# Stage order and buffer depth in the edge score stage of a graph network kernel

## Chip, cores and metric

One core of one Trainium2 chip runs the whole kernel. The metric is device time in microseconds (us) of one execution; the number compared is the median of repeated runs.

## What is computed

The reference takes 50,000 nodes of 128 features and 25,000 edges through four graph layers. The part that matters here is the start of the third layer, an edge attention:

```python
x_norm = _layernorm(x, g1, be1)
q = (x_norm @ Wq + bq).reshape(num_nodes, NH, HD)
k = (x_norm @ Wk + bk).reshape(num_nodes, NH, HD)
v = (x_norm @ Wv + bv).reshape(num_nodes, NH, HD)
scores = jnp.einsum('ehd,ehd->eh', q[src], k[tgt]) / np.sqrt(HD).astype(np.float32)
scores = scores + (curv @ Wc + bc)
```

There are 8 heads of 16 features. `curv` is the edge attribute table, 25,000 rows of 128. The kernel fetches both end rows of each edge and does norm and projections per edge; nothing is computed per node and looked up later.

## The kernel before

The stage is `scores_phase` (L2301 to L2477). The edges are padded to 200 tiles of 128 and taken in 50 groups of four tiles (`GT = 4`, `EG = 50`). Each group goes through these steps:

- **Gather** (L2378, POOL): eight indirect DMAs fetch the source and the target rows of four tiles, each row in two halves of 128 features, into one of four slots (`SC = 4`) of `sc_rows`. Gather g waits until group g-4 has been added.
- **Add** (L2393, DVE): the halves are added into `sc_xin`, and `norm.statistics` (L1150 to L1163) makes mean and variance.
- **Root** (L1171, ACT), then **normalise** (L1176, L1183, DVE): reciprocal and eight tensor_scalar into `sc_xn`.
- **Turn** (L2448, L2450, PE): eight 128x128 transposes of `sc_xn` and four of the attribute rows, into three PSUM tiles `sc_t`. Then PE waits for its own transposes (L2452) and gives the attribute slot free (L2453).
- **Copy** (L2423, L2424, ACT): the three PSUM tiles go to SBUF.
- **Project** (L2473, L2463, L2467, PE): three biases and twelve 128x128 matmuls into query, key and value PSUM tiles `sc_o`, and the small attribute product. There is one set of these tiles, so project g+1 waits until group g is scored and its value is copied.
- **Values** (L2429, L2431, ACT): copy of query and of value.
- **Score** (L2403, L2406, L2409, DVE): query times key, sum by head, plus the attribute part.
- **Load and put** (L2343, L2359, SP): 256 KB of attribute rows in, 256 KB of values out. The attribute rows have two slots.

What sets the order is written out by hand. `pipeline` (L1883) runs ticks m = 0, 1, 2, and so on; in tick m each engine's program does its steps in the listed order, step s for group m minus the lag of s. Each engine then runs its list strictly in order, and semaphores join the engines. In the kernel before the lists are:

- DVE: normalise (lag 1), score (3), add (0)
- ACT: values (3), copy (1), root (0)
- PE: turn (1), project (2)
- SP: load (0), put (4)

After its own steps each engine also does a piece of `EdgeEnds` (L2480 to L2580) in its tick: small loads of ids and bias rows on SP in ticks 0 to 9, the filling of a table with bias rows from tick 12 on (two 512 KB DMAs per tick), and some masks on DVE, ACT and PE. The change leaves these as they are.

Of the kernel before, what the change touches and what calls it, by code (L numbers as in the profile page):

```python
# [20 lines left out]
P = 128  # L21
D = 128
# [2277 lines left out]

def scores_phase(k, o, ends):  # L2301
# [4 lines left out]
    with ExitStack() as st:  # L2306
        rows = k.sb(st, "sc_rows", [P, SC, C, 2 * D])
        attr = k.sb(st, "sc_attr", [P, 2, GT, D])
# [12 lines left out]
        names = ["attr0", "attr1", "attr_tail", "attr_free", "added", "normed", "turned", "copied",  # L2321
# [9 lines left out]
        def run(*stages):  # L2331
            pipeline(EG, *((lambda g, f=f: f(g, g // 2, g % 2, P), lag) for f, lag in stages))

        with nc.Block() as block:
            @block.sync
            def _(sp):
                edge_attr = k.a["edge_attr_128"]

                def load(g, i, u, p):
                    sp.wait_ge(s["attr_free"], g + 1)  # L2340
                    if not isinstance(g, int) or g < full:
                        at = slice(g * (GT * P), (g + 1) * (GT * P)) if isinstance(g, int) else bass.ds(g * (GT * P), GT * P)
                        sp.dma_start(attr[:, u, :, :], edge_attr[at, :].rearrange("(t p) d -> p t d", p=P))\  # L2343
                          .then_inc(s[f"attr{u}"], 16)
                    elif g == full:
# [6 lines left out]
                                     .rearrange("(t p) d -> p t d", p=P)).then_inc(s[f"attr{u}"], 16)  # L2352
                    else:
                        sp.sem_inc(s[f"attr{u}"], 16)

                def put(g, i, u, p):
                    sp.wait_ge(s["value"], g + 2)
                    at = slice(g * (GT * P), (g + 1) * (GT * P)) if isinstance(g, int) else bass.ds(g * (GT * P), GT * P)
                    sp.dma_start(k.values[at, 0:D].rearrange("(t p) d -> p t d", p=P), value[:, u, :, :])\  # L2359
                      .then_inc(s[f"value_put{u}"], 16)  # L2360

                sp.wait_ge(s["cleared"], 1)
                for u in range(2):
                    sp.sem_inc(s[f"value_put{u}"], 16)
                run((load, 0), (put, 4), (lambda g, i, u, p: ends.sync(g), 0))
                ends.close_sync()
                for u in range(2):
                    sp.wait_ge(s[f"value_put{u}"], 16 * (EG // 2) + 16)
# [15 lines left out]
            def _(dve):  # L2384
# [3 lines left out]
                dve.sem_inc(s["scored"], 1)  # L2388

                def add(g, i, u, p):  # L2390
# [7 lines left out]
                def normalise(g, i, u, p):  # L2398
                    norm.normalise(dve, g, u, P, xn[:, u, :, :], xin[:, u, :, :]).then_inc(s["normed"], 1)
# [1007 lines left out]
```

## Time and profile before

| what | value |
|---|---|
| median of 3 runs | 5611.9 us |
| lowest and highest | 5609.29 and 5619.23 us |
| span of the profiled execution | 5967.4 us |
| PE busy, share of the span | 3527.0 us, 59% |
| DVE busy, share | 3844.7 us, 64% |
| ACT busy, share | 2300.9 us, 39% |
| POOL busy, share | 3031.0 us, 51% |
| mean granted TensorE clock | 0.792 |

The span goes from the first to the last instruction. For the profiled execution no other time than its span is recorded; it is 355.5 us, or 6.3%, above the median of the runs without a profile. The busy shares are means over stages that differ, so they don't tell what bounds any one stage. The score stage takes from 2828.7 us to about 3526 us of the span, 12% of it.

### The profile page before, as it was taken

The numbers are of one execution on the slowest core, as the hardware profiler recorded it, in microseconds if no ns is written. First come the engines' busy times: TensorE is split into PE (matmuls) and PEld (weight loads), VectorE is DVE, ScalarE is ACT, GpSimd is POOL, SyncE is SP. The second block draws the span as 40 slices with busy tenths as digits, with TensorE's granted clock in tenths as the row PEclk, the third lists the DMA queues.
The fourth block names the chain that finished last, engine by engine and source line by source line (L and its number), as shares of the span: only waits on it lengthen the run. The fifth ranks groups of instructions, "written<-read, shape, count | busy, mean of one in ns | idle before, by whom it ended". The sixth has DMA issues, their size and how long they took to land. (4 is left out here: it accounts for less than half of the span.)

```text
span 5967.4 us, 70027 instructions
## 1 busy us (share of the span) xinstructions
PE 3527.0 (59%) x19808; PEld 2717.4 (46%) x19808; DVE 3844.7 (64%) x11203; ACT 2300.9 (39%) x5320; POOL 3031.0 (51%) x2733
## 2 busy tenths in 40 slices
PE   5677766267712466631455644444799993775443
PEld 1344445267611255531355542333577772664443
DVE  9666568379835466621465566666678882666998
ACT  0233330068810255521122222333466662334776
POOL 8666557625567422376655516776155555552000
PEclk9898887689955688965677776766899996997666
DMA  4455559479857777621455427777356653775554
GB/s 181 125 150 153 151 146 331 143 227 310 273 163 265 254 244 248 229 84 55 122 188 194 149 52 212 241 245 226 143 204 212 211 209 99 235 244 196 208 209 160
DMA packets 698336, 1147.11 MB, mean 192 GB/s; under 512 B 110368, under 2 KB 453459, under 8 KB 691702
## 3 DMA queue, kind: packets, MB, share of 16 engines
q1 hardware_dynamic: 594752, 959.48, 48.6%
q0 software_dynamic: 103200, 183.16, 10.5%
q8 instruction: 162, 2.65, 0.2%
q14 instruction: 222, 1.82, 0.1%
HBM read 689.93 MB, written 464.79 MB: 194 GB/s over the span
## 5 line engine op out<-in xcount | busy, mean ns | idle before, releaser
L2378 POOL DMA_INDIRECT sc_rows<-layer,node_idx x400 | 385.1, 963 | 264.3 <-DVE sc_xin L2393 135.6
L2252 PE MATMUL ro_end<-vals,end_mask 128*2 128x128 f32 x1600 | 243.0, 317 | 388.4 <-DVE vals L2116 243.2
L778 PE MATMUL msg_acc<-msg_pair,msg_vals 128*128 128x512 f32 (+3 forms) x400 | 210.2, 699 | 310.8 <-issue 147.5
L2903 POOL DMA_INDIRECT tf_edge_x<-y,tf_src_idx x200 | 198.0, 990 | 382.9 <-SPq L2879 334.2
L208 POOL DMA_INDIRECT x_src<-in_x_dram,node_idx x200 | 329.7, 1649 | 81.6 <-issue 60.7
L3049 PE MATMUL tf_o_ps<-pre_w,tf_hidden 128*128 128x128 f32 (+1 forms) x3136 | 362.2, 276 | 5.8 <-issue 5.2
L2252 PEld LDWEIGHTS ro_end<-vals,end_mask 128*2 128x2 f32 x1600 | 148.3, 96 | 474.0 <-DVE vals L2116 252.0
L3037 PE MATMUL tf_h_ps<-tf_x_t,pre_w 128*128 128x512 f32 x784 | 350.2, 600 | 19.1 <-ACT tf_hidden L2997 18.0
L3049 PEld LDWEIGHTS tf_o_ps<-pre_w,tf_hidden 128*128 128x128 f32 (+1 forms) x3136 | 356.6, 192 | 7.7 <-issue 7.6
L2278 PE MATMUL ro_acc<-vals,ro_mask 128*126 128x128 f32 x1600 | 240.4, 314 | 201.6 <-ACT ro_square L2210 87.0
L1611 POOL DMA_INDIRECT cap_own<-layer,w_own x200 | 204.5, 1022 | 292.2 <-SPq L1591 242.1
L2997 ACT ACTIVATE tf_hidden<-tf_h_ps,pre_b 128x512 f32<-128x512 f32 x392 | 269.1, 687 | 159.5 <-PE tf_h_ps L3037 119.3
L401 POOL DMA_INDIRECT agg<-rank_sums,d_last x200 | 211.5, 1058 | 227.0 <-ACT rank_sums L494 173.5
L2278 PEld LDWEIGHTS ro_acc<-vals,ro_mask 128*126 128x126 f32 x1600 | 222.3, 223 | 223.4 <-issue 188.3
L2066 POOL TENSOR_TENSOR vals<-ro_both,ro_weight 126x1024 f32<-126x1024 f32 x75 | 145.0, 1933 | 344.1 <-ACT ro_weight L2234 258.7
L1114 PE MATMUL ml_conv_out<-pre_mean_wt,ml_conv_tsb 128*128 128x128 f32 (+1 forms) x784 | 176.6, 417 | 231.4 <-DVEq L3221 226.8
L698 POOL DMA_INDIRECT msg_rows<-values,s_eid x200 | 217.9, 1090 | 186.9 <-POOLq L70 126.2
L778 PEld LDWEIGHTS msg_acc<-msg_pair,msg_vals 128*128 128x128 f32 x400 | 115.7, 304 | 402.8 <-issue 247.2
L893 POOL DMA_INDIRECT agg<-mean_sums,d_last x200 | 208.7, 1043 | 177.4 <-ACT mean_sums L938 128.3
L1114 PEld LDWEIGHTS ml_conv_out<-pre_mean_wt,ml_conv_tsb 128*128 128x128 f32 (+1 forms) x784 | 164.8, 319 | 244.5 <-issue 238.7
L1521 POOL DMA_INDIRECT sorted<-payload,rank x200 | 233.0, 1165 | 77.5 <-issue 64.2
L2079 POOL DMA_INDIRECT layer<-ro_far,w_last x200 | 215.8, 1079 | 105.0 <-issue 60.0
(487 smaller groups left out, 11220.1 us busy)
## 6 DMA issues: line engine op xcount, KB each, us to landing
ro_mask<-masks SPq DMA_DIRECT2D x100, 504.0 KB
layer<-zeros SPq DMA_DIRECT2D x96, 512.0 KB
si_both<-layer SPq DMA_DIRECT2D x48, 1024.0 KB
ro_far<-far SPq DMA_DIRECT2D x75, 512.0 KB
ro_both<-both SPq DMA_DIRECT2D x75, 512.0 KB
agg<-zeros SPq DMA_DIRECT2D x48, 512.0 KB
mom_x<-in_x_dram SPq DMA_DIRECT2D x48, 512.0 KB
mom_agg<-agg SPq DMA_DIRECT2D x48, 512.0 KB
```

The lines of the kernel that those rows point to most:

```text
L208: k.nc.gpsimd.indirect_dma_start(out=rows[:, t, :], out_offset=None, in_=k.x, in_offset=bass.IndirectOffsetOnAxis(ap=k.node_idx[:, 0, t:t ...
L698: nc.gpsimd.indirect_dma_start(out=rows[:, g % SS, j, :], out_offset=None, in_=table, in_offset=bass.IndirectOffsetOnAxis(ap=order.eid[:, ...
L778: mm = nc.tensor.matmul(acc[g % 3][:, i:GT, :].rearrange("p t e -> p (t e)"), vals[:, u, i, :], pair[:, u, FIRST[i]:FIRST[i] + GT - i, :]. ...
L1114: mm = self.k.nc.tensor.matmul(self.out[b][0:p, j, :], self.turned_sb[:, 4 * b + j, 0:p], self.weight, start=plain, stop=plain or j == 3, ...
L1521: k.nc.gpsimd.indirect_dma_start(out=k.sorted4[:, :], out_offset=bass.IndirectOffsetOnAxis(ap=k.rank[:, t:t + 1], axis=0), in_=k.payload[: ...
L2079: nc.gpsimd.indirect_dma_start(out=k.layer1_halves, out_offset=bass.IndirectOffsetOnAxis(ap=wide.last[real, t:t + 1], axis=0), in_=sent[re ...
L2252: mm = nc.tensor.matmul(end_ps[0:2, j, :], k.end_mask[:, t, :], k.vals[:, t, :], start=True, stop=True, skip_group_check=True)
L2278: mm = nc.tensor.matmul(acc[w][real, j, :], mask[:, u, j, :], k.vals[:, tile(n, j), :], start=True, stop=True, skip_group_check=True)
L2378: nc.gpsimd.indirect_dma_start(out=rows[:, g % SC, c * GT + j, :], out_offset=None, in_=k.layer1, in_offset=bass.IndirectOffsetOnAxis(ap=k ...
L2997: nc.scalar.activation(hidden[:, h, b, :], h_ps[b][:, :], ACT.Relu, bias=b1[:, b:b + 1]).then_inc(s["bent"], 1)
L3037: nc.tensor.matmul(h_ps[b][:, :], w1[:, b * P:(b + 1) * P], x_t[:, u, 4 * h:4 * h + 4, :].rearrange("p j e -> p (j e)"), start=True, stop= ...
L3049: mm = nc.tensor.matmul(o_ps[h][0:p, j, :], hidden[:, h, b, j * P:j * P + p], w2[:, b, :], start=b == 0, stop=b == NB - 1)
```

## The change

It touches only `scores_phase`. The lags become: DVE normalise 1, score 4, add 0; ACT values 4, copy 2, root 0; PE turn 2, project 3; SP load 0, put 5. So a group is turned in the tick after that in which it was normalised, and projected in the one after that. The attribute rows get four slots (`AS = 4`) with a semaphore each. A load now waits on `turned` directly, so PE's wait for its own transposes and the semaphore `attr_free` go. Normalise g gets a wait for turn g-2, which the old order implied; score also waits for `made`. Counts that were preset at the start (`value`, `copied`, `made`, `scored`, `value_put`) now start at zero.

```diff
--- before.py
+++ after.py
@@ -2298,6 +2298,9 @@
 Q = NH * CH
 
 
+AS = 4
+
+
 def scores_phase(k, o, ends):
 
 
@@ -2305,7 +2308,7 @@
     C = 2 * GT
     with ExitStack() as st:
         rows = k.sb(st, "sc_rows", [P, SC, C, 2 * D])
-        attr = k.sb(st, "sc_attr", [P, 2, GT, D])
+        attr = k.sb(st, "sc_attr", [P, AS, GT, D])
         xin = k.sb(st, "sc_xin", [P, 2, C, D])
         xn = k.sb(st, "sc_xn", [P, 2, C, D])
         x_t = k.sb(st, "sc_x_t", [P, 2, C, P])
@@ -2318,7 +2321,7 @@
         t_ps = [k.ps(st, f"sc_t{b}", [P, GT, P]) for b in range(3)]
         out_ps = [k.ps(st, f"sc_o{b}", [P, GT, D]) for b in range(3)]
         attr_ps = k.ps(st, "sc_attr_ps", [P, 512])
-        names = ["attr0", "attr1", "attr_tail", "attr_free", "added", "normed", "turned", "copied",
+        names = ["attr_in0", "attr_in1", "attr_in2", "attr_in3", "attr_tail", "added", "normed", "turned", "copied",
                  "made", "query", "value", "value_put0", "value_put1", "product", "dots", "scored", "cleared"]
         s = {x: k.sem(st, "sc_" + x) for x in names}
         ends.begin(st)
@@ -2328,20 +2331,18 @@
         full = E // (GT * P)
         assert full % 2 == 0 and full + 2 == EG
 
-        def run(*stages):
-            pipeline(EG, *((lambda g, f=f: f(g, g // 2, g % 2, P), lag) for f, lag in stages))
-
         with nc.Block() as block:
             @block.sync
             def _(sp):
                 edge_attr = k.a["edge_attr_128"]
 
-                def load(g, i, u, p):
-                    sp.wait_ge(s["attr_free"], g + 1)
-                    if not isinstance(g, int) or g < full:
-                        at = slice(g * (GT * P), (g + 1) * (GT * P)) if isinstance(g, int) else bass.ds(g * (GT * P), GT * P)
-                        sp.dma_start(attr[:, u, :, :], edge_attr[at, :].rearrange("(t p) d -> p t d", p=P))\
-                          .then_inc(s[f"attr{u}"], 16)
+                def load(g):
+                    u = g % AS
+                    if g >= AS:
+                        sp.wait_ge(s["turned"], g - AS + 1)
+                    if g < full:
+                        sp.dma_start(attr[:, u, :, :], edge_attr[g * (GT * P):(g + 1) * (GT * P), :]
+                                     .rearrange("(t p) d -> p t d", p=P)).then_inc(s[f"attr_in{u}"], 16)
                     elif g == full:
 
                         at, left = full * GT * P, E - full * GT * P
@@ -2349,23 +2350,20 @@
                           .then_inc(s["attr_tail"], 16)
                         sp.wait_ge(s["attr_tail"], 16)
                         sp.dma_start(attr[:, u, 0:left // P, :], edge_attr[at:at + left // P * P, :]
-                                     .rearrange("(t p) d -> p t d", p=P)).then_inc(s[f"attr{u}"], 16)
+                                     .rearrange("(t p) d -> p t d", p=P)).then_inc(s[f"attr_in{u}"], 16)
                     else:
-                        sp.sem_inc(s[f"attr{u}"], 16)
-
-                def put(g, i, u, p):
-                    sp.wait_ge(s["value"], g + 2)
-                    at = slice(g * (GT * P), (g + 1) * (GT * P)) if isinstance(g, int) else bass.ds(g * (GT * P), GT * P)
-                    sp.dma_start(k.values[at, 0:D].rearrange("(t p) d -> p t d", p=P), value[:, u, :, :])\
-                      .then_inc(s[f"value_put{u}"], 16)
+                        sp.sem_inc(s[f"attr_in{u}"], 16)
+
+                def put(g):
+                    sp.wait_ge(s["value"], g + 1)
+                    sp.dma_start(k.values[g * (GT * P):(g + 1) * (GT * P), 0:D].rearrange("(t p) d -> p t d", p=P),
+                                 value[:, g % 2, :, :]).then_inc(s[f"value_put{g % 2}"], 16)
 
                 sp.wait_ge(s["cleared"], 1)
-                for u in range(2):
-                    sp.sem_inc(s[f"value_put{u}"], 16)
-                run((load, 0), (put, 4), (lambda g, i, u, p: ends.sync(g), 0))
+                pipeline(EG, (load, 0), (put, 5), (ends.sync, 0))
                 ends.close_sync()
                 for u in range(2):
-                    sp.wait_ge(s[f"value_put{u}"], 16 * (EG // 2) + 16)
+                    sp.wait_ge(s[f"value_put{u}"], 16 * (EG // 2))
 
             @block.gpsimd
             def _(pool):
@@ -2385,78 +2383,78 @@
                 norm.prepare(dve)
                 nc.vector.memset(attr[:, :, :, :], 0.0).then_inc(s["cleared"], 1)
                 dve.wait_ge(s["cleared"], 1)
-                dve.sem_inc(s["scored"], 1)
-
-                def add(g, i, u, p):
-                    q = g % SC
+
+                def add(g):
+                    q, u = g % SC, g % 2
                     dve.wait_ge(k.gathered[q], in0[q] + (g // SC + 1) * 32 * GT)
                     nc.vector.tensor_tensor(xin[:, u, :, :], rows[:, q, :, 0:D], rows[:, q, :, D:2 * D],
                                             ALU.add).then_inc(s["added"], 1)
                     dve.wait_ge(s["added"], g + 1)
                     norm.statistics(dve, g, u, P, xin[:, u, :, :])
 
-                def normalise(g, i, u, p):
-                    norm.normalise(dve, g, u, P, xn[:, u, :, :], xin[:, u, :, :]).then_inc(s["normed"], 1)
-
-                def score(g, i, u, p):
+                def normalise(g):
+                    if g >= 2:
+                        dve.wait_ge(s["turned"], g - 1)
+                    norm.normalise(dve, g, g % 2, P, xn[:, g % 2, :, :], xin[:, g % 2, :, :]).then_inc(s["normed"], 1)
+
+                def score(g):
                     dve.wait_ge(s["query"], g + 1)
+                    dve.wait_ge(s["made"], g + 1)
                     nc.vector.tensor_tensor(terms[:, :, :], query[:, :, :], out_ps[1][:, :, :],
                                             ALU.mult).then_inc(s["product"], 1)
                     dve.wait_ge(s["product"], g + 1)
                     nc.vector.tensor_reduce(dots[:, :, :], terms[:, :, :].rearrange("p t (h d) -> p t h d", h=NH),
                                             AX.X, ALU.add).then_inc(s["dots"], 1)
                     dve.wait_ge(s["dots"], g + 1)
-                    nc.vector.tensor_tensor(k.scores[:, slice(g * GT, g * GT + GT) if isinstance(g, int) else bass.ds(g * GT, GT), :],
-                                            dots[:, :, :],
+                    nc.vector.tensor_tensor(k.scores[:, g * GT:(g + 1) * GT, :], dots[:, :, :],
                                             attr_ps[:, 0:GT * NH].rearrange("p (t h) -> p t h", h=NH),
                                             ALU.add).then_inc(s["scored"], 1)
 
-                run((normalise, 1), (score, 3), (add, 0), (lambda g, i, u, p: ends.vector(g), 0))
+                pipeline(EG, (normalise, 1), (score, 4), (add, 0), (ends.vector, 0))
 
             @block.scalar
             def _(act):
-                def copy(g, i, u, p):
+                def copy(g):
+                    u = g % 2
                     act.wait_ge(s["turned"], g + 1)
-                    if g:
-                        act.wait_ge(s["made"], g)
+                    if g >= 2:
+                        act.wait_ge(s["made"], g - 1)
                     for b in range(2):
                         nc.scalar.activation(x_t[:, u, b * GT:(b + 1) * GT, :], t_ps[b][:, :, :], ACT.Copy)
                     nc.scalar.activation(attr_t[:, u, :, :], t_ps[2][:, :, :], ACT.Copy).then_inc(s["copied"], 1)
 
-                def values(g, i, u, p):
-                    act.wait_ge(s["made"], g + 2)
-                    act.wait_ge(s["scored"], g + 1)
+                def values(g):
+                    u = g % 2
+                    act.wait_ge(s["made"], g + 1)
+                    if g:
+                        act.wait_ge(s["scored"], g)
                     nc.scalar.activation(query[:, :, :], out_ps[0][:, :, :], ACT.Copy).then_inc(s["query"], 1)
-                    act.wait_ge(s[f"value_put{u}"], i * 16 + 16)
+                    if g >= 2:
+                        act.wait_ge(s[f"value_put{u}"], g // 2 * 16)
                     nc.scalar.activation(value[:, u, :, :], out_ps[2][:, :, :], ACT.Copy).then_inc(s["value"], 1)
 
-                act.sem_inc(s["copied"], 1)
-                act.sem_inc(s["value"], 1)
-                run((values, 3), (copy, 1), (lambda g, i, u, p: norm.square_root(act, g, u, p), 0),
-                    (lambda g, i, u, p: ends.scalar(g), 0))
+                pipeline(EG, (values, 4), (copy, 2), (lambda g: norm.square_root(act, g, g % 2, P), 0), (ends.scalar, 0))
 
             @block.tensor
             def _(pe):
-                pe.sem_inc(s["made"], 1)
-                pe.sem_inc(s["attr_free"], 2)
-
-                def turn(g, i, u, p):
+                def turn(g):
+                    u, q = g % 2, g % AS
                     pe.wait_ge(s["normed"], g + 1)
-                    pe.wait_ge(s["copied"], g + 1)
-                    pe.wait_ge(s[f"attr{u}"], i * 16 + 16)
+                    if g:
+                        pe.wait_ge(s["copied"], g)
+                    pe.wait_ge(s[f"attr_in{q}"], g // AS * 16 + 16)
                     for j in range(C):
                         nc.tensor.transpose(t_ps[j // GT][:, j % GT, :], xn[:, u, j, :], k.ident[:, :])
                     for j in range(GT):
-                        mm = nc.tensor.transpose(t_ps[2][:, j, :], attr[:, u, j, :], k.ident[:, :])
+                        mm = nc.tensor.transpose(t_ps[2][:, j, :], attr[:, q, j, :], k.ident[:, :])
                     mm.then_inc(s["turned"], 1)
-                    pe.wait_ge(s["turned"], g + 1)
-                    pe.sem_inc(s["attr_free"], 1)
-
-                def project(g, i, u, p):
-                    pe.wait_ge(s["copied"], g + 2)
-
-                    pe.wait_ge(s["value"], g + 1)
-                    pe.wait_ge(s["scored"], g + 1)
+
+                def project(g):
+                    u = g % 2
+                    pe.wait_ge(s["copied"], g + 1)
+                    if g:
+                        pe.wait_ge(s["value"], g)
+                        pe.wait_ge(s["scored"], g)
                     for c in range(3):
                         add_bias(out_ps[c][:, :, :].rearrange("p t d -> p (t d)"), k.qkv_parts[c])
                         for j in range(GT):
@@ -2473,7 +2471,7 @@
                     nc.tensor.matmul(out, k.ones_bias[:, :], parts[:, :, :].rearrange("r t d -> r (t d)"), start=True,
                                      stop=False, skip_group_check=True)
 
-                run((turn, 1), (project, 2), (lambda g, i, u, p: ends.tensor(g), 0))
+                pipeline(EG, (turn, 2), (project, 3), (ends.tensor, 0))
         clear_semaphores(nc, norm.sems + list(s.values()) + ends.sems)
```

## Rows read from the trace of the kernel before

**Rows 1.** Busy time by engine (microseconds, instructions), granted clock, DMA share, score stage.

```profile
core 0: us, PE busy (x) PEld busy (x) DVE busy (x) ACT busy (x) POOL busy (x), PEclk, DMA share, GB/s
2835.00:3520.00 685.00, 390.28 (x2384) 354.34 (x2385) 379.64 (x1366) 150.77 (x302) 380.70 (x396) 0.74 0.49 153
```

**Rows 2.** The add of the two row halves: duration in ns, first and last start.

```profile
L2393 DVE TENSOR_TENSOR sc_xin<-sc_rows x50: 1216/1217/1226, 2840.9 to 3500.5; 128x1024 f32<-128x1024 f32 x50
```

**Rows 3.** Table of waits in the stage: total microseconds, times, longest.

```profile
ACT sc_query L2429 <- remote: 250.7, 34, 17.4
...
POOL sc_rows L2378 <- DVE sc_xin L2393: 135.6, 26, 11.8
...
PE sc_o L2473 <- remote: 117.3, 21, 9.1
```

**Rows 4.** Timeline: two gathers on POOL, eight apart (start, duration).

```profile
2833.21 0.95 POOL L2378 DMA_INDIRECT sc_rows<-layer,node_idx  x1 [0.30 <-issue]
...
2843.23 0.95 POOL L2378 DMA_INDIRECT sc_rows<-layer,node_idx  x1 [0.30 <-issue]
```

**Rows 5.** Timeline, middle of the stage: three groups on PE, ACT and DVE.

```profile
3278.40 1.08 ACT L2423 ACTIVATE sc_x_t<-sc_t 128x512 f32<-128x512 f32 x2 [5.32 <-remote]
...
3278.67 0.59 PE L2473 MATMUL sc_o<-pre_query_parts,ones_bias 128*128 128x512 bf16 x1 [6.73 <-remote]
...
3280.43 2.14 DVE L1183 TENSOR_SCALAR sc_xn<-sc_xin,sc_norm_mean,sc_norm_scale 128x128 f32<-128x128 f32 x8
...
3287.82 0.60 ACT L2429 ACTIVATE sc_query<-sc_o 128x512 f32<-128x512 f32 x1 [7.66 <-remote]
...
3288.94 1.08 ACT L2423 ACTIVATE sc_x_t<-sc_t 128x512 f32<-128x512 f32 x2
...
3290.00 1.22 DVE L2393 TENSOR_TENSOR sc_xin<-sc_rows 128x1024 f32<-128x1024 f32 x1
...
3290.23 0.59 PE L2473 MATMUL sc_o<-pre_query_parts,ones_bias 128*128 128x512 bf16 x1 [1.32 <-DVE scores L2409]
...
3297.57 0.60 PE L2450 MATMUL sc_t<-ident,sc_attr 128*128 128x128 f32 x4
...
3298.59 0.60 ACT L2429 ACTIVATE sc_query<-sc_o 128x512 f32<-128x512 f32 x1 [4.45 <-remote]
...
3304.29 1.08 ACT L2423 ACTIVATE sc_x_t<-sc_t 128x512 f32<-128x512 f32 x2 [4.61 <-remote]
...
3304.56 0.58 PE L2473 MATMUL sc_o<-pre_query_parts,ones_bias 128*128 128x512 bf16 x1 [6.39 <-remote]
...
3314.41 0.60 ACT L2429 ACTIVATE sc_query<-sc_o 128x512 f32<-128x512 f32 x1 [8.37 <-remote]
```

**Rows 6.** Timeline, end of the stage, after the last gather.

```profile
3492.53 1.22 DVE L2393 TENSOR_TENSOR sc_xin<-sc_rows 128x1024 f32<-128x1024 f32 x1
...
3492.76 0.38 PE L2473 MATMUL sc_o<-pre_query_parts,ones_bias 128*128 128x512 bf16 x1 [0.54 <-DVE scores L2409]
...
3497.18 0.60 ACT L2429 ACTIVATE sc_query<-sc_o 128x512 f32<-128x512 f32 x1 [0.51 <-PE sc_attr_ps L2467]
...
3500.06 0.60 PE L2450 MATMUL sc_t<-ident,sc_attr 128*128 128x128 f32 x4
...
3500.53 1.22 DVE L2393 TENSOR_TENSOR sc_xin<-sc_rows 128x1024 f32<-128x1024 f32 x1
3500.70 1.09 ACT L2423 ACTIVATE sc_x_t<-sc_t 128x512 f32<-128x512 f32 x2 [2.43 <-PE sc_t L2450]
```

**Rows 7.** Timeline, start of the stage: cleared rows, first turn, adds two and three.

```profile
2828.97 0.91 DVE L2386 MEMSET sc_attr<- 128x1024 f32 x1 [0.19 <-issue]
...
2850.73 1.06 PE L2450 MATMUL sc_t<-ident,sc_attr 128*128 128x128 f32 x4
...
2855.10 1.08 ACT L2423 ACTIVATE sc_x_t<-sc_t 128x512 f32<-128x512 f32 x2 [10.03 <-remote]
...
2861.26 1.23 DVE L2393 TENSOR_TENSOR sc_xin<-sc_rows 128x1024 f32<-128x1024 f32 x1 [0.92 <-DMA sc_rows<-layer,node_idx]
...
2910.07 1.22 DVE L2393 TENSOR_TENSOR sc_xin<-sc_rows 128x1024 f32<-128x1024 f32 x1
```

**Rows 8.** Stretch view, end of the stage, columns as in rows 1.

```profile
3490.00:3507.00 17.00, 12.15 (x99) 11.23 (x99) 15.31 (x58) 7.01 (x14) 0.00 (x0) 1.00 0.11 32
```

## The prediction

> **What bounds the stage now.** I read the stretch view first, for the whole stage. Over 685 us PE is busy 390 us, DVE 380 us, POOL 381 us and ACT 151 us [rows 1]: no engine is near full, so the stage is bound by waits between engines. Then the period (groups are counted from 0). The first and the last of 50 adds start at 2840.9 and 3500.5 us [rows 2]. Add 3 starts at 2910.07 us [rows 7] and add 48 at 3492.53 us [rows 6], so 45 ticks take 582.5 us. The last two of them and the one after fall in the part without gathers, where a tick takes 8.0 to 8.4 us (3492.53 to 3500.53 us is one of 8.0 [rows 6]). That leaves 43 ticks of about (582.5 - 16.4) / 43 = 13.2 us while gathers run.
>
> Two floors lie below 13.2. POOL needs 10.0 us for eight gathers when nothing stops it (2833.21 to 2843.23 us [rows 4]). DVE is busy 380 / 50 = 7.6 us a group [rows 1], and that is why the quiet ticks take 8.0. The table of waits says the same from the other side: POOL stood 135.6 us waiting for the add, ACT 250.7 us before the query copy, PE 117.3 us before a projection [rows 3]. "Remote" is a semaphore that rose when no instruction was recorded as ending. The timeline shows what that is. In the quiet part the last transposes of a turn end by their record at 3500.66 us and ACT copies them at 3500.70 us [rows 6]. In the middle the same records end at 3298.17 us and the copy starts at 3304.29 us, 6.1 us later [rows 5]; in the first turn it is 2851.79 to 2855.10 us, 3.3 us, though PE had nothing else to do [rows 7]. So as long as gathers run, PE's results are reported 3 to 6 us late.
>
> The loop that sets 13.2 can be followed over two ticks [rows 5]. A projection starts at 3278.67 us, its query is copied from 3287.82 us, the score is done and the next add starts at 3290.00 us, the group of that add is normalised in the next tick, turned, copied at 3304.29 us, and only then does PE start the projection at 3304.56 us, since the turn stands ahead of it in PE's list. That is 25.9 us for two ticks. In this loop the turn's late report is paid in full, because normalise and turn of a group stand in one tick.
>
> **What the change does to a tick.** Turn g+2 uses a group that was normalised a tick earlier, so PE goes from project g to turn g+2 without waiting for DVE, and to project g+1 without waiting for its own transposes. The new loop is project, query copy, score, next project:
>
> - Project start to query copy: 3278.67 to 3287.82 us is 9.15, 3290.23 to 3298.59 us is 8.36, 3304.56 to 3314.41 us is 9.85 [rows 5]; mean 9.1 us.
> - Query copy to next project: 3287.82 to 3290.23 us, 2.4 us [rows 5].
> - The turn that lies beside this: from the query copy to the copy of the turned tiles it took 1.1 us (3287.82 to 3288.94) and 5.7 us (3298.59 to 3304.29) [rows 5]. Where it is really work and above 2.4 us, it delays the next project, since PE works in order. Between the ends I take 2.9 us for the larger of the two, nearer to the row that hides it.
>
> Sum: 9.1 + 2.9 = 12.0 us, against 13.2. The ends are 10.0 us (POOL's floor) and no gain at all. 43 ticks times 1.2 us are 52 us.
>
> **What it adds.** The lists are one tick longer, and at the end this tick is not covered: in the quiet part it costs 8.0 us [rows 6]. Clearing four attribute slots in place of two doubles a memset of 0.9 us [rows 7], +0.9 us, on the path before the first load. Normalise waits for turn g-2. Behind that wait on DVE are score and add, and for them wait PE and POOL; turn g-2 follows project g-4, and DVE comes to this wait only after score g-4 and add g, over 6 us after that projection, so it costs nothing unless a turn is later than that (the 5.7 us above is close). Root g on ACT stands behind copy g-2 in place of copy g-1, with the same margin. The attribute slots cost and gain nothing: the loads waited for PE, and PE's turn in no row for a load. On SP the load of a tick waits for a turn two ticks older, so it and what follows it (put, the table filling) go out no later than before; the put is one tick down the list but its group is too. POOL's list is unchanged, it only gets its slots back earlier. The start, where adds 2 and 3 lie 48.8 us apart [rows 7], has no known cause; I leave it as it is, with up to one tick either way.
>
> Against its own time the sum is 5967.4 - 52 + 8 + 1 = 5924 us, -43 us. **From there to the median.** The profiled execution took 355.5 us, 6.3%, longer than the median, and I cannot place that. The late reports may belong to the recording: in the steady part I find them only at PE, which leaves the most records, and only while gathers run. If they are wholly so, the tick of the plain runs is near POOL's 10.0 already and the change is worth +9 us; if not at all, -43 us. I take a bit over half of the way: **-27 us, 5585 us**. My own range for this case is 5565 to 5600 us.
>
> **A rule against the row.** By the granted clock, which is 0.74 over the stage and 1.00 at its quiet end [rows 1, 8], PE runs the middle at a mix of 1.2 and 2.4 GHz. A projection takes 4.4 us at the end (3492.76 to 3497.18 us [rows 6]) and 9.1 us in the middle. The Trainium skill, page "TensorE: Matmul & The Clock Gate", section "HAM oscillation", says that pauses of PE between bursts make the clock fall, so a list without pauses would keep it at the upper level. By that rule the projection would come near 4.4 us and POOL's 10.0 us would set the tick. The row at the start speaks against it: a first turn with an idle PE was 3.3 us late too, which no clock explains.
>
> **Rivals.**
>
> 1. *The stage falls to POOL's floor.* Project 4.4 + 2.9 us would be below 10.0, so the tick is 10.0: 43 x 3.2 - 9 = 129 us in the profile, between 50 and 100 in the median, 5512 to 5560 us. For it: the quiet ticks of 8.0 us. Against it: PE's reports are late whatever PE does. Chance 0.12.
> 2. *Nothing in the steady part, only the drain.* The plain runs are already at POOL's floor, or PE really works from project to turn without a pause, which the order does not shorten. For it: in the rows turned tiles are followed by the next project within 0.3 us (3304.29 to 3304.56), and the excess of the profile. Time: 5612 to 5621 us. Chance 0.26. The case that the attribute slots were the aim and do nothing is within this one.
> 3. *Slower: the turn comes to stand between two projects.* Place: PE's list, turn ahead of project, both ready at once. Before, the turn could begin only when DVE was done and part of its lateness lay beside DVE's work; now all of it can lie in line, and root, normalise and score shift with it. Price: with the 5.7 us of the rows a tick is 9.1 + 5.7 + 0.3 = 15.1 us, +1.9 x 43 + 9 = +91 us in the profile; it decides from a turn of over 3.8 us after the projection. With 4.7 us: 43 x 0.9 + 9 = +48 us in the profile, half of that or all in the median, 5636 to 5660 us. For it: a turn of 5.7 us is in the rows. Against it: that turn's input came only 2 us before the projection ended, so part of the 5.7 is not PE's. Chance 0.14.
>
> **How the numbers follow.** The forecast case has 0.48, and nearly all of it (0.45) lies under 5600.7 us. The bound for faster or slower is 0.2%, 11.2 us, about what a measurement of this kernel can tell from no change. Faster: 0.45 + 0.12 = 0.57. Within: the rest of the forecast case and most of rival 2, 0.27. Slower: rival 3 and the upper edge of rival 2, 0.16. The range 5535 to 5635 us takes in the forecast case, rival 2, and the near halves of 1 and 3.
>
> **What would show it.** In the profile after: adds 12.0 us apart in the middle (10.0: rival 1; 13.2: rival 2; 14 and more: rival 3). PE's project should start about 2.4 us after the query copy of the group before and no longer right after the copy of the turned tiles. POOL's wait for the add should fall from 135.6 us by about 50. The waits of the query copy should stay, since the projection itself is not shorter. The stage should end one tick of 8 us later after the last gather. The forecast is wrong if the period falls in the profile and the median stays (the late reports were the recording's), or if the period does not fall and project follows the turned tiles as before.

## The result, and the profile after

The changed kernel is slower: 5632.29 us median of 10 runs (5624.07 to 5639.57) against 5616.11 us for the kernel before, also 10 runs (5609.29 to 5623.55). The ratio is 1.0028, with a 95% interval of 1.002 to 1.0036, so +16 us. The forecast was 5585 us, a gain.

The profile of before on which the prediction rests is of an execution 6% longer than any plain run, and its score stage runs differently, not only slower. A second profile of the same kernel (experiment e1) has a span of 5614.9 us and stands here for "before"; the profile of the changed kernel has 5622.3 us. What made the first one long stays open.

The first lines of the changed kernel's page:

```profile
span 5622.3 us, 70067 instructions
## 1 busy us (share of the span) xinstructions
PE 3431.4 (61%) x19808; PEld 2669.7 (47%) x19808; DVE 3836.0 (68%) x11203; ACT 2294.5 (41%) x5320; POOL 2951.2 (52%) x2733
```

The stretch view of the whole score stage, first for before (e1), then for the changed kernel; the columns are those of [rows 1]:

```profile
2674.00:3219.00 545.00, 367.34 (x2404) 335.54 (x2404) 383.75 (x1371) 153.13 (x305) 391.36 (x400) 0.81 0.63 194
```

```profile
2675.00:3232.00 557.00, 352.37 (x2404) 328.69 (x2404) 384.31 (x1370) 150.21 (x305) 399.22 (x400) 0.81 0.62 190
```

The stage takes 545 us in place of the 685 us of [rows 1], and DVE is busy for the same 384 us. The table of waits over the stage tells who sets the pace (total, times, longest). Before (e1):

```profile
PEld sc_t L2448 <- DVE sc_xn L1183: 237.1, 49, 95.9
...
ACT sc_x_t L2423 <- PE sc_t L2450: 184.1, 50, 6.8
POOL sc_rows L2378 <- issue: 121.6, 399, 0.3
DVE sc_xin L2393 <- DMA sc_rows<-layer,node_idx: 113.3, 49, 11.1
```

The changed kernel:

```profile
ACT sc_norm_root L1171 <- DVEq L1163: 350.1, 50, 16.0
PE sc_o L2471 <- DVE scores L2409: 173.0, 49, 9.3
...
POOL sc_rows L2376 <- issue: 121.6, 399, 0.3
DVE sc_xin L2390 <- DMA sc_rows<-layer,node_idx: 114.1, 41, 11.3
PEld sc_t L2447 <- DVE sc_xn L1183: 105.7, 3, 97.5
```

A landing is the moment at which a DMA's rows have arrived. In neither does POOL wait for DVE: the line of 135.6 us in [rows 3] is gone, and all POOL stands idle for is its own issue, 121.6 us. DVE waits for landed gathers, in 49 of 50 adds before and in 41 after. Both kernels are bound by POOL's gathers, and PE waits in both: before it waits for the normalised rows in 49 ticks, as the old order says, and after that wait is gone (3 left) and stands as a wait for the score (49). The reorder did what it says, on an engine that wasn't the bound. There is no "remote" of the kind of [rows 3] on top of either table.

The group view of the gathers (count, busy time, mean ns, idle before), before (e1) and after:

```profile
L2378 POOL DMA_INDIRECT sc_rows<-layer,node_idx x400 | 391.4, 978 | 128.9 <-issue 121.6 <-POOLq L70 7.3
```

```profile
L2376 POOL DMA_INDIRECT sc_rows<-layer,node_idx x400 | 399.2, 998 | 128.9 <-issue 121.6 <-POOLq L70 7.3
```

Here are the first 8 us: the same 400 gathers take 391.4 us before and 399.2 us after, with the same idle time. From the start of the first to the end of the last it is 512.9 against 520.8 us. The rest is at the end. Last gather, last add, last score of before (e1):

```profile
3186.63 0.95 POOL L2378 DMA_INDIRECT sc_rows<-layer,node_idx  x1 [0.30 <-issue]
...
3193.37 1.22 DVE L2393 TENSOR_TENSOR sc_xin<-sc_rows 128x1024 f32<-128x1024 f32 x1 [6.07 <-DMA sc_rows<-layer,node_idx]
...
3218.23 0.19 DVE L2409 TENSOR_TENSOR scores<-sc_dots,sc_attr_ps 128x32 f32<-128x32 f32 x1
```

and of the changed kernel:

```profile
3195.14 0.95 POOL L2376 DMA_INDIRECT sc_rows<-layer,node_idx  x1 [0.30 <-issue]
...
3201.61 1.22 DVE L2390 TENSOR_TENSOR sc_xin<-sc_rows 128x1024 f32<-128x1024 f32 x1 [5.61 <-DMA sc_rows<-layer,node_idx]
...
3231.50 0.19 DVE L2409 TENSOR_TENSOR scores<-sc_dots,sc_attr_ps 128x32 f32<-128x32 f32 x1
```

From the end of the last gather to the end of the last score it is 30.8 us before and 35.6 us after. Together the stage is 12.6 us longer in these two profiles, within the interval of the measured 16 us.

**Where gathers get long.** Most gathers take 0.95 us in both. In the changed kernel 29 take over 1.3 us, and 25 of these start while DVE adds; before it is 10, and 6 of them. Summed over all gathers, what they take beyond 0.946 us each is 20.8 us in the changed kernel, 17.5 of it in gathers that start during an add, and 13.0 us before, 6.8 of it there. So the 7.9 us more on POOL are +10.7 us beside the adds and -2.8 us beside DVE's other work (its normalise, up to 1.03 us a gather, and the id work of `EdgeEnds`, four gathers of over 1.3 us in each kernel). A timeline of the changed kernel, with SP's DMAs, shows one:

```profile
3008.70 0.37 SPq L2359 DMA_DIRECT2D values<-sc_value  x1
3009.11 1.04 SPq L2520 DMA_DIRECT2D msum<-ee_bo_rows  x2
...
3010.20 1.08 SPq L2344 DMA_DIRECT2D sc_attr<-in_edge_attr_dram  x1
...
3010.55 0.95 POOL L2376 DMA_INDIRECT sc_rows<-layer,node_idx  x1 [0.30 <-issue]
...
3015.55 0.94 POOL L2376 DMA_INDIRECT sc_rows<-layer,node_idx  x1 [0.30 <-issue]
...
3016.41 1.23 DVE L2390 TENSOR_TENSOR sc_xin<-sc_rows 128x1024 f32<-128x1024 f32 x1 [6.26 <-DMA sc_rows<-layer,node_idx]
3016.79 1.67 POOL L2376 DMA_INDIRECT sc_rows<-layer,node_idx  x1 [0.30 <-issue]
```

SP issues its burst from 3008.70 us on: values out, two fillings of the table, attribute rows in, 1.5 MB together. The last gather of the group is issued at 3010.55 us and the add waits 6.26 us for landing, until 3016.41 us. The gather that starts at 3016.79 us, 0.38 us into the add, takes 1.67 us: it ends 0.82 us after the add's end (3017.64 us). A tick of before (e1):

```profile
3003.12 0.95 POOL L2378 DMA_INDIRECT sc_rows<-layer,node_idx  x1 [0.30 <-issue]
...
3003.38 0.38 SPq L2343 DMA_DIRECT2D sc_attr<-in_edge_attr_dram  x1
...
3003.81 0.53 SPq L2359 DMA_DIRECT2D values<-sc_value  x1
...
3004.37 0.95 POOL L2378 DMA_INDIRECT sc_rows<-layer,node_idx  x1 [0.30 <-issue]
3004.38 1.05 SPq L2522 DMA_DIRECT2D msum<-ee_bo_rows  x2
3004.60 1.22 DVE L2393 TENSOR_TENSOR sc_xin<-sc_rows 128x1024 f32<-128x1024 f32 x1 [1.89 <-DMA sc_rows<-layer,node_idx]
...
3005.62 1.02 POOL L2378 DMA_INDIRECT sc_rows<-layer,node_idx  x1 [0.30 <-issue]
```

Here SP's burst goes out with the add, the gather at 3004.37 us started 0.23 us before the add and takes 0.95 us, and the next, 1.02 us into the add, takes 1.02 us.

Over all adds this is one line: a gather that starts d us after the start of an add of 1.22 us takes 2.04 - d us for d from 0.07 to 1.1, and 0.95 us if it started before the add or within 0.04 us of its start. So each add can cost POOL between 0 and 1.0 us, depending on the phase. And the phase is set by landing for the most part. In groups 12 to 43 the add starts 2.5 to 2.9 us after the start of its group's last gather in 27 of 32 cases before (mean 2.9 us); after, in 5 of 32 (2.7 to 7.1 us, mean 4.3 us). By the semaphores that tell of the landings, the last rows of a group are there 2.85 us before and 4.04 us after, in the mean, counted in the same way; that is 1.2 of the 1.4 us. The rest is DVE itself: in 8 of the 32 groups of the changed kernel it comes to the add 0.3 to 1.9 us after the landing, before in one (0.5 us). Why it is late there was not separated.

### The profile page after: what moved, and what is told of

Same layout as the page of the kernel before. It is cut to its first block and busy times, and to the rows that moved or that the text cites. A ratio compares the mean times of both kernels' runs of the same rounds, so it can differ in the third digit from the quotient of the medians.

```text
span 5622.3 us, 70067 instructions
## 1 busy us (share of the span) xinstructions
PE 3431.4 (61%) x19808; PEld 2669.7 (47%) x19808; DVE 3836.0 (68%) x11203; ACT 2294.5 (41%) x5320; POOL 2951.2 (52%) x2733
## 5 line engine op out<-in xcount | busy, mean ns | idle before, releaser
L2376 POOL DMA_INDIRECT sc_rows<-layer,node_idx x400 | 399.2, 998 | 128.9 <-issue 121.6
L208 POOL DMA_INDIRECT x_src<-in_x_dram,node_idx x200 | 231.5, 1157 | 81.9 <-issue 59.3
L2053 POOL DMA_INDIRECT ro_far<-layer,w_far x200 | 226.5, 1133 | 87.5 <-issue 59.9
```

What stands on the lines that cost most here:

```text
L208: k.nc.gpsimd.indirect_dma_start(out=rows[:, t, :], out_offset=None, in_=k.x, in_offset=bass.IndirectOffsetOnAxis(ap=k.node_idx[:, 0, t:t ...
L2053: nc.gpsimd.indirect_dma_start(out=far[real, u, j, :], out_offset=None, in_=k.layer1_halves, in_offset=bass.IndirectOffsetOnAxis(ap=wide.f ...
L2376: nc.gpsimd.indirect_dma_start(out=rows[:, g % SC, c * GT + j, :], out_offset=None, in_=k.layer1, in_offset=bass.IndirectOffsetOnAxis(ap=k ...
```

## Experiments

**e1, before, second profile.** No edit.

> The kernel before, unchanged, for a second profile. The profile of the changed kernel has a span of 5622.3 us, near its runs, while the first profile of before had 5967.4. Theory A (both kernels are at POOL's floor of gathers while these run, and only the end of the stage got longer): span near 5615 us, adds about 10.4 us apart, DVE waiting for landed gathers in most groups, and from the last gather to the last score about 27 us, one tick of 8 us less than the 35.6 us of the changed kernel. Theory B (the new order slows the part with gathers): the same 35 us at the end, but the gathers spread over clearly less than the 520.8 us of the changed kernel, by 16 us or so.

Measured: 5616.66 us in its one run, span 5614.9 us. Adds 10.2 us apart in the median and 10.3 us in the mean in the middle (groups 12 to 43), 30.8 us at the end, gathers in 512.9 us: the lines above. Both theories have a part: A in that POOL is the floor and the end got longer, B in that the gathers are 8 us shorter than in the changed kernel.

**e2, two attribute slots under the new order.**

```diff
-AS = 4
+AS = 2
```

> The changed kernel with two attribute slots in place of four, all lags and semaphores as changed. If the slots cost (longer clearing memset, more DMA in flight beside the gathers), this is faster than the changed kernel, down to the time before (ratio to before 1.000). If the lags are the cause, slots do nothing: ratio to before 1.002 to 1.004. If attribute rows would come late without four slots, it is slower still, over 1.005.

Measured: ratio to before 1.0039 (1.0027 to 1.0052). Gathers in 520.4 us, POOL busy 398.9 us, end 40.8 us. The slots are not the cause, and nothing shows that the new order needs them.

**e3, old lags under the new semaphores.**

```diff
-pipeline(EG, (load, 0), (put, 5), (ends.sync, 0))
+pipeline(EG, (load, 0), (put, 4), (ends.sync, 0))
-pipeline(EG, (normalise, 1), (score, 4), (add, 0), (ends.vector, 0))
+pipeline(EG, (normalise, 1), (score, 3), (add, 0), (ends.vector, 0))
-pipeline(EG, (values, 4), (copy, 2), ...
+pipeline(EG, (values, 3), (copy, 1), ...
-pipeline(EG, (turn, 2), (project, 3), (ends.tensor, 0))
+pipeline(EG, (turn, 1), (project, 2), (ends.tensor, 0))
```

> The changed kernel with the old lags (normalise 1, score 3, values 3, copy 1, turn 1, project 2, put 4), but four slots and the new semaphores without PE's wait for its own transposes. If the lags are the cause: ratio to before 1.000, at best 0.999 for the wait that is gone. If slots or semaphores are the cause: 1.002 to 1.004.

Measured: 1.0028 (1.0017 to 1.0039). The end is short again (30.0 us), but the gathers take 524.6 us and POOL is busy 403.1 us. So the lags cause the longer end, and the longer gathers have another cause, which e2 and e3 share with the changed kernel. What all three have is the place of SP's burst. The put of the values starts 6.3, 5.8 and 6.2 us after an add in the mean of groups 12 to 43 (the changed kernel, e2, e3); before it starts 0.6 us ahead of one. SP's own waits over the stage, for before (e1), the changed kernel and e2, show what holds the burst back:

```profile
SPq L2343 <- PEq L2453: 390.6, 46, 19.9
```

```profile
SPq L2359 <- ACT sc_value L2434: 431.9, 50, 15.4
```

```profile
SPq L2344 <- PE sc_t L2449: 401.4, 45, 20.1
```

Before, the load waits for a turn whose rows were normalised in the same tick, and the burst then goes out beside the next add. In the changed kernel, and in e3 in the same way (437.1 us), that wait is all but gone (5.7 us) and the put waits for its value. In e2 the load still waits for a turn, but under the new lags the turns come at another place of the tick, about 5 us after an add.

**e4 and e5, POOL relieved, under the old and the new order.** The target rows come by one plain load on SP, for which the add waits too; the scores are computed from other target rows.

```diff
+def near(g):
+    if g >= SC:
+        sp.wait_ge(s["added"], g - SC + 1)
+    sp.dma_start(rows[:, g % SC, GT:2 * GT, :],
+                 k.layer1[g * (GT * P):(g + 1) * (GT * P), :].rearrange("(t p) d -> p t d", p=P))\
+      .then_inc(s[f"near{g % SC}"], 16)
...
-for c in range(2):
+for c in range(1):
```

> The kernel before with POOL relieved: the four gathers of the target rows of each group are replaced by one plain load of 512 consecutive rows on the SP queue, so POOL's floor falls from 10.0 to about 5 us a group. The target rows, and with them the scores, are other numbers. If POOL's floor bounds the stage, it gets shorter by up to 50 x (10.4 - 8) = 120 us, down to DVE's 8.0 us a tick or to the loop of project, score, add, normalise and turn; ratio to before about 0.98 to 0.99. If PE or the loop bounds it already, the ratio stays near 1.00.

> The changed kernel with POOL relieved in the same way. If the new order takes the turn out of the loop and this loop was only hidden by POOL's floor, this is faster than the relieved kernel before, by up to 1 us a tick, 50 us. If DVE's 8.0 us sets the tick of both, the two are alike but for the longer end, 8 to 16 us slower. If the turn stands between projections, it is slower by more than 20 us.

Measured: 0.9814 (0.9792 to 0.9836) for the old order, 0.9832 (0.9811 to 0.9852) for the new one. The adds (duration, first and last start), old order, then new:

```profile
L2401 DVE TENSOR_TENSOR sc_xin<-sc_rows x50: 1209/1217/1226, 2681.8 to 3089.3; 128x1024 f32<-128x1024 f32 x50
```

```profile
L2398 DVE TENSOR_TENSOR sc_xin<-sc_rows x50: 1216/1216/1226, 2689.0 to 3094.0; 128x1024 f32<-128x1024 f32 x50
```

With POOL out of the way the stage loses 100 us, so POOL's floor bounds it. Adds 3 to 45 come 8.3 us apart under both orders, and DVE is busy for 317 and 316 of the 350 us from 2700 to 3050 us: its floor, or near it. The loop through the turn, which I had blamed, doesn't bind even here, since the order makes no difference. The last score ends 23.8 us after the start of the last add in e4 and 31.7 us in e5: the extra tick, 7.9 us.

**e6 and e7, SP's burst put back behind the add,** under the old lags (e3) and the new ones (the changed kernel):

```diff
 def load(g):
     u = g % AS
     if g >= AS:
         sp.wait_ge(s["turned"], g - AS + 1)
+    if g:
+        sp.wait_ge(s["added"], g)
```

> The kernel e3 (old lags, four slots, new semaphores) with one wait more on SP: the load of group g waits until group g-1 is added, as it did in effect in the kernel before, so that SP's bursts (load, put, table filling, 1.25 MB) start just after an add. Theory P (phase): in e3 and in the changed kernel the bursts fall before the landing of a group's last gather, the landing varies, adds start at any phase of POOL's running gather, and a gather that starts during an add is held until the add's end plus 0.8 us (about 25 to 30 gathers of over 1.3 us against 10 in the kernel before). Then this goes back to the kernel before: POOL busy 391 us in the stage, gathers over 513 us, ratio 1.000 (e3: 1.0028). Rival N (the bursts have nothing to do with it, PE's missing wait or chance sets the phase): POOL busy stays at 399 to 403 us and the ratio at 1.002 to 1.003.

> The changed kernel with the same wait on SP. Theory P: the gathers take 513 us in place of 521, only the longer end is left, 5 to 8 us; ratio 1.001. Rival N: as the changed kernel, 1.003.

Measured: e6 1.0000 (0.999 to 1.0009), e7 1.0017 (1.0008 to 1.0026). The gathers of e6, then of e7:

```profile
L2378 POOL DMA_INDIRECT sc_rows<-layer,node_idx x400 | 390.3, 976 | 128.9 <-issue 121.5 <-POOLq L70 7.3
```

```profile
L2378 POOL DMA_INDIRECT sc_rows<-layer,node_idx x400 | 389.9, 975 | 128.9 <-issue 121.5 <-POOLq L70 7.3
```

One wait brings POOL back to 390 us and the gathers to 511.8 and 511.4 us, and the add comes 2.5 to 2.9 us after the last gather's start in 22 and 21 of the 32 groups. What is left of e7 is its end, 39.4 against 31.5 us. Theory P (the place of the bursts) holds and N falls. The burst is 1.5 MB, and not the 1.25 MB of the expectation.

**e10, the opposite: the burst made late in the kernel before.**

```diff
 sp.wait_ge(s["attr_free"], g + 1)
+if g:
+    sp.wait_ge(s["normed"], g)
```

> The kernel before with one wait more on SP: the load of group g waits until group g-1 is normalised, so that SP's bursts fall 6 to 8 us after an add, where they fell in the changed kernel, and end near the landing of the next group. Lags, slots and semaphores are those of before. Theory P: the cost of the changed kernel appears in the kernel before: more than 20 gathers over 1.3 us, POOL busy about 399 us in place of 391, ratio about 1.0015. Rival N (the place of the bursts is not the cause): POOL busy 391 us, ratio 1.000.

Measured: 1.0029 (1.0018 to 1.0041), 26 gathers over 1.3 us, 22 of them started during an add, gathers in 521.7 us, end 32.2 us. Group view and two ticks:

```profile
L2380 POOL DMA_INDIRECT sc_rows<-layer,node_idx x400 | 400.1, 1000 | 128.9 <-issue 121.5 <-POOLq L70 7.3
```

```profile
2989.94 1.23 DVE L2395 TENSOR_TENSOR sc_xin<-sc_rows 128x1024 f32<-128x1024 f32 x1 [0.67 <-DMA sc_rows<-layer,node_idx]
2990.17 1.81 POOL L2380 DMA_INDIRECT sc_rows<-layer,node_idx  x1 [0.30 <-issue]
...
2996.66 0.38 SPq L2345 DMA_DIRECT2D sc_attr<-in_edge_attr_dram  x1
2997.09 0.51 SPq L2361 DMA_DIRECT2D values<-sc_value  x1
...
2997.64 1.04 SPq L2524 DMA_DIRECT2D msum<-ee_bo_rows  x2
...
2999.79 0.95 POOL L2380 DMA_INDIRECT sc_rows<-layer,node_idx  x1 [0.30 <-issue]
...
3002.95 1.23 DVE L2395 TENSOR_TENSOR sc_xin<-sc_rows 128x1024 f32<-128x1024 f32 x1 [4.83 <-DMA sc_rows<-layer,node_idx]
...
3003.54 1.45 POOL L2380 DMA_INDIRECT sc_rows<-layer,node_idx  x1 [0.30 <-issue]
```

The burst goes out from 2996.66 us on, the add waits until 3002.95 us, and gathers at 2990.17 and 3003.54 us are held (1.81 and 1.45 us). With lags, slots and semaphores of before, the place of the burst alone makes POOL's 8.8 us. The ratio is above what these 10 us of the stage give (1.0018); the interval reaches down to it.

**e8 and e9, each add in four pieces,** in the kernel before and in the changed one:

```diff
-nc.vector.tensor_tensor(xin[:, u, :, :], rows[:, q, :, 0:D], rows[:, q, :, D:2 * D], ALU.add).then_inc(s["added"], 1)
+for h in range(4):
+    ins = nc.vector.tensor_tensor(xin[:, u, 2 * h:2 * h + 2, :], rows[:, q, 2 * h:2 * h + 2, 0:D],
+                                  rows[:, q, 2 * h:2 * h + 2, D:2 * D], ALU.add)
+ins.then_inc(s["added"], 1)
```

> The kernel before with each add cut into four adds of two tiles (about 0.33 us each). If a gather is held by the instruction in flight, it now gets in between the pieces: POOL busy falls from 391 us toward 380 (400 x 0.946 = 378), ratio 0.998 to 0.999. If the hold lasts as long as adds follow each other, nothing changes: 1.000.

> The changed kernel with each add cut in four. If the hold is by instruction, most of the 21 us of held gathers go: POOL busy from 399 toward 382 us, ratio to before 0.999 to 1.000, which is 0.3% faster than the changed kernel. If not: 1.003.

Measured: e8 0.9996 (0.9987 to 1.0005), e9 1.0003 (0.9994 to 1.0012). The gathers of e8, of e9, and a piece of e8's timeline:

```profile
L2378 POOL DMA_INDIRECT sc_rows<-layer,node_idx x400 | 387.6, 969 | 128.9 <-issue 121.6 <-POOLq L70 7.3
```

```profile
L2376 POOL DMA_INDIRECT sc_rows<-layer,node_idx x400 | 387.4, 968 | 128.9 <-issue 121.6 <-POOLq L70 7.3
```

```profile
2993.81 0.94 POOL L2378 DMA_INDIRECT sc_rows<-layer,node_idx  x1 [0.30 <-issue]
...
2994.01 1.43 DVE L2394 TENSOR_TENSOR sc_xin<-sc_rows 128x256 f32<-128x256 f32 x4 [1.60 <-DMA sc_rows<-layer,node_idx]
...
2995.06 1.19 POOL L2378 DMA_INDIRECT sc_rows<-layer,node_idx  x1 [0.30 <-issue]
```

The four pieces take 1.43 us, and the gather that starts 1.05 us into them takes 1.19 us, as if only the last piece had held it. POOL is busy 387.6 and 387.4 us, the gathers take 509.1 and 509.0 us, with only 4 and 3 over 1.3 us and none of these in an add, though the adds of e9 are as scattered as in the changed kernel (mean 4.3 us after the last gather's start). So the hold, and not the late landing itself, is what costs POOL time. What the changed kernel keeps is its end (39.8 us).

**e11 and e12, shorter lists.** e11 is e6 with a group's add, normalise, turn, copy and project in one tick; e12 is e11 with the add in four pieces.

```diff
-pipeline(EG, (load, 0), (put, 4), (ends.sync, 0))
+pipeline(EG, (load, 0), (put, 2), (ends.sync, 0))
-pipeline(EG, (normalise, 1), (score, 3), (add, 0), (ends.vector, 0))
+pipeline(EG, (add, 0), (normalise, 0), (score, 1), (ends.vector, 0))
-pipeline(EG, (values, 3), (copy, 1), (lambda g: norm.square_root(act, g, g % 2, P), 0), (ends.scalar, 0))
+pipeline(EG, (lambda g: norm.square_root(act, g, g % 2, P), 0), (values, 1), (copy, 0), (ends.scalar, 0))
-pipeline(EG, (turn, 1), (project, 2), (ends.tensor, 0))
+pipeline(EG, (turn, 0), (project, 0), (ends.tensor, 0))
```

> The kernel e6 (bursts just after an add) with shorter lists in place of longer ones: add, normalise, turn, copy and project of a group in one tick, values and score in the next. One group then takes from landing about 1.2 (add) + 2.7 (statistics) + 0.6 (root) + 2.3 (normalise) + 2 (turn) + 1.8 (copy) + 5.5 (project) + 2.4 (query, score) = 18.5 us, and a tick of 10.1 us still hides it. Theory: as POOL sets the tick, only the end of the stage depends on the lags: from the last gather to the last score about 20 us in place of 31, the gathers in 512 us; ratio 0.998. Rival: in one tick the chain is too long, POOL waits for adds; then gathers over 520 us and ratio over 1.000.

> The kernel e11 with each add cut in four. Gathers in 509 us and the short end: ratio 0.9975. If the two gains don't add, as e11.

Measured: e11 1.0008 (0.9998 to 1.0018), e12 0.9976 (0.9965 to 0.9986). e11 missed: its end is short (25.5 us, not 20), but its gathers take 521.2 us. The reason is the same mechanism, by my own hand: with `put` two ticks behind, SP waits for a value, and the put starts 5 to 11 us after an add, so values and filling go out late again. In e12 the pieces take the sting out of that:

```profile
L2378 POOL DMA_INDIRECT sc_rows<-layer,node_idx x400 | 386.6, 966 | 128.9 <-issue 121.6 <-POOLq L70 7.3
```

Gathers in 508.1 us, end 26.0 us. e12 is 0.24% faster than the kernel before, and by the two ratios (0.9976 / 1.0028) 0.5% faster than the changed one.

## Why the prediction was wrong

**What bounds the stage: wrong.** The step that failed is the first. I took 13.2 us a tick and late reports of PE from one profile that was 6% longer than the runs, and built on it the loop project, score, add, normalise, turn, project, which was to bind while gathers run. In the second profile a tick is 10.3 us in the mean, 512.9 us of gathers for 50 groups, against POOL's floor of 10.0 us. POOL waits for nothing but its own issue, and that is the bound. I had written that the tick of the plain runs might be near POOL's 10.0 and that the change would then be worth +9 us; I still put the forecast "a bit over half of the way" to -43 us (from +9 us, -27 us is even 69% of it). The 355.5 us that I could not place should have stopped me from forecasting by that loop at all: [rows 4] with 10.0 us for eight gathers, times 50, was a bound that held in both profiles.

**The term of 43 ticks times 1.2 us (-52 us): measured 0.** With POOL relieved the tick is 8.3 us under either order (e4, e5), so the turn is in no loop that binds, with or without POOL's floor.

**The longer end (+8 us): right.** Five kernels with the old lags end 30.0 to 32.2 us after the last gather (e1, e3, e6, e8, e10; mean 31.3), four with the new ones 35.6 to 40.8 us (the changed kernel, e2, e7, e9; mean 38.9): +7.6 us. e7 against e6 has it alone, 7.9 us.

**SP and POOL cost nothing: wrong, and this is about half of the 16 us;** the longer end is the rest. The prediction says of the load that "it and what follows it (put, the table filling) go out no later than before". It asked whether the DMAs go out late, not what they meet. They go out at another phase of the tick, 6 us after an add in place of with it, and there they delay the landing of the last gather by 1.2 us in the mean; the adds lose their fixed place between two gathers, and the gathers that start during an add are held. POOL's list is unchanged and its time is not: +7.9 us. e3 and e10 show the cost under the old lags (+11.7 and +8.8 us on POOL), e6 and e7 take it away. Rival 2 had the right bound and only the drain, +8 to +9 us; with POOL's 8 us, and counted from the 5616.11 us measured beside it, that is 5632 us, as measured.

**The slots, the memset and the wait for turn g-2: right, as far as can be told.** e2 has two slots and is no faster. The memset takes 1.76 in place of 0.91 us, the +0.9 us of the sum. In the changed kernel normalise waited for PE's turn once in the whole stage, for 0.5 us.

**The Trainium skill's rule on the clock** (the one that the prediction sets against its row) was not put to the test: PE pauses in the changed kernel too, 173.0 us before the projections alone, and its granted clock is 0.81 over the stage in both kernels. While gathers run, POOL is the bound, and PE's clock is not part of the time.

**Rival 3** (the turn stands between two projections) did not come about: PE waits for the score in 49 ticks of the changed kernel, by which time the turn is done.

## What to carry to other kernels

If the profiled execution is several per cent off the plain runs, use only what must hold in both: an engine's count of instructions times their undisturbed duration is such a floor, a loop of waits is not. When the order of a list changes, follow each DMA issue to its new place in the tick and ask what lands then, even if the queue has time to spare. And where the bound is an engine that shares something with another, the phase between them is part of the cost; here one wait that pins the phase took e3 from 1.0028 to 1.0000 (e6), and an add cut into short pieces took the changed kernel from 1.0028 to 1.0003 (e9).

## What the runs showed of the hardware that was not expected

- A GpSimd gather (DMA_INDIRECT) that starts while VectorE adds two SBUF operands is held until the end of that add plus 0.82 us (durations up to 1.97 us in place of 0.95 us). One that started more than 0.02 us before the add is not held, and the add takes its 1.22 to 1.23 us. Where the two start together, the gather from 0.02 us before to 0.04 us after the add's start, it is the add that gets longer, 1.24 to 1.30 us, and the gather takes its 0.95 us (13 times in the changed kernel, e2, e3, e10 and e11).
- The Trainium skill, page "SBUF — State Buffer", section "Who interferes with whom", says that a VectorE instruction with two SBUF inputs contends, through a shared read interface, with a GpSimd instruction that reads SBUF. The trace agrees for a gather that comes second (1.67 us in the timeline above). The page also says that whoever issues first keeps the shared ports for the whole instruction, but it says so of VectorE's 2-port modes, and not of this add. Here a gather that starts together with the add makes it up to 0.08 us longer, and one that started earlier doesn't hold it, though each runs for 0.95 us.
- That the pieces of e8 hold a gather only for the piece in flight fits this; that it is the gather's first access to SBUF that is held is an inference from the constant 0.82 us, not shown. The same 0.82 us stands behind a comparison of two SBUF operands in `EdgeEnds` (L2535, 1.89 us, in e1): the gather that starts 0.91 us into it takes 1.80 us.
- SP's burst before a landing moves it from 2.85 to 4.04 us in the mean and up to 7.1 us. Whether the queue, the DMA engines or the memory is what they share was not separated.
- Why the first profile of before was 6% longer, with reports of PE 3 to 6 us late, stays open; no other profile showed it.
